# Turned keys masked for all four heads of a tile in one GpSimd operation, and a pipeline with one turn less

## The reference

```
scale, shift = split(cond @ W_emb + b_emb)
xn = rms_norm(x, g_norm) * (1 + scale) + shift
q, k, v = xn @ W_qkv              # 16 heads of 16
q, k = rms_norm(q, g_q), rms_norm(k, g_k)
o = softmax(q k^T / 4) v          # within each sequence, 32 x 32
x = x + o + o @ W_out
```

```
r, z = sigmoid(x W_ir + b + h W_hr + b), sigmoid(x W_iz + b + h W_hz + b)
n = tanh(x W_in + b + r * (h W_hn + b))
h = (1 - z) * n + z * h;  out = x + h
```

## Time and profile before

| | |
|---|---|
| median of 3 runs | 341.93 us (341.85 to 342.36) |
| profiled execution, first to last instruction | 340.0 us |
| attention stage in it, up to the first recurrent product | 191.54 us |
| TensorE, VectorE, ScalarE, GpSimd busy | 323.3, 246.3, 238.0, 224.5 us |

### The profile page before, as it was taken

How to read it: one execution, slowest core, us unless ns; L and a number is a source line. 1 busy time by engine, 2 the same in 40 slices (tenths; PEclk the granted TensorE clock), 3 DMA queues, 4 the chain that set the end, 5 groups by cost and what they waited for, 6 DMA issues and landing times.

```text
span 340.0 us, 12168 instructions
## 1 busy us (share of the span) xinstructions
PE 323.3 (95%) x4177; PEld 293.4 (86%) x4177; DVE 246.3 (72%) x665; ACT 238.0 (70%) x722; POOL 224.5 (66%) x404
## 2 busy tenths in 40 slices
PE   8988899899999999999986999999999999999994
PEld 8767788788888888888874999999999999999994
DVE  3778898888999999999996455565555556555555
ACT  4787777778888788889656566666666666666662
POOL 6787787867777877878778346555555555555542
PEclk9999999999999999999999999999999999999999
DMA  5965237742343333233332221111112111122221
GB/s 202 307 193 151 86 76 234 226 132 85 109 121 113 101 114 99 86 117 116 112 109 65 80 77 48 61 49 62 62 62 62 48 58 50 62 62 62 63 62 33
DMA packets 32205, 34.14 MB, mean 100 GB/s; under 512 B 5286, under 2 KB 26796, under 8 KB 32172
## 3 DMA queue, kind: packets, MB, share of 16 engines
q1 hardware_dynamic: 25868, 26.10, 25.6%
q10 hardware_dynamic: 6304, 7.61, 7.0%
HBM read 12.46 MB, written 8.39 MB: 61 GB/s over the span
## 4 chain that ended last, share of the span: by engine, by line
PE 78%; POOL 7%; SPq 4%; DMA 4%; issue 3%; DVE 3%; ACT 1%; POOLq 0%; DVEq 0%; ACTq 0%
PE bank L1287 38%; PE bank L1244 19%; PE bank L1400 4%; PE bank L1419 4%; PE bank L1388 4%; DMA operands<-operands 4%; PE bank L1531 3%; SPq L414 2%; POOL operands L485 2%; PE bank L1380 2%; SPq L405 2%; PE bank L1250 2%; PE bank L1371 2%; POOL xn L496 1%; POOL xn_lo L531 1%
## 5 line engine op out<-in xcount | busy, mean ns | idle before, releaser
L1287 PE MATMUL bank<-wih_lo,wo_parts 128*128 128x256 f32 x192 | 56.2, 294 | 0.0
L1287 PE MATMUL bank<-wih_hi,wo_parts 128*128 128x256 f32 x192 | 54.6, 285 | 0.2 <-POOL pair_lo L600 0.2
L1287 PE MATMUL bank<-wih_hi,pair_lo 128*128 128x256 f32 x192 | 52.8, 279 | 0.0
L1287 PE MATMUL bank<-wqkv_hi,hT_hi 128*128 128x256 f32 x192 | 52.5, 292 | 0.0
L611 POOL TENSOR_TENSOR operands<-operands,h 128x128 f32<-128x128 f32 x64 | 29.6, 462 | 34.2 <-ACT operands L932 33.4
L1287 PE MATMUL bank<-wqkv_lo,hT_hi 128*128 128x256 f32 x192 | 49.9, 279 | 0.0
L1187 DVE TENSOR_TENSOR operands<-bank,operands 128x128 f32<-128x128 f32 x64 | 18.6, 291 | 39.3 <-ACT operands L929 39.3
L1244 PE MATMUL bank<-wqkv_hi,xn_hi 128*128 128x512 f32 (+1 forms) x124 | 46.4, 375 | 0.2 <-POOL xn_lo L531 0.2
L618 POOL TENSOR_TENSOR w_emb_sb<-h,w_emb_sb 128x256 f32<-128x256 f32 x31 | 22.9, 737 | 30.7 <-DVE h L1204 30.7
L1287 PE MATMUL bank<-wqkv_hi,hT_lo 128*128 128x256 f32 x192 | 42.7, 279 | 0.0
L1244 PE MATMUL bank<-wqkv_hi,xn_lo 128*128 128x512 f32 (+1 forms) x124 | 41.9, 338 | 0.0
(11 more groups left out here) (138 smaller groups left out, 975.2 us busy)
## 6 DMA issues: line engine op xcount, KB each, us to landing
v_diag<-v_rows SPq DMA_DIRECT2D x124, 34.0 KB, 2.1
operands<-operands SPq DMA_DIRECT2D x32, 128.0 KB, 2.1
out_dram<-x ACTq DMA_DIRECT2D x16, 256.0 KB, 2.6
w_emb_sb<-out_dram SPq DMA_DIRECT2D x32, 128.0 KB, 2.1
operands<-operands SPq DMA_DIRECT2D x63, 64.0 KB, 2.0
out_dram<-w_emb_sb SPq DMA_DIRECT2D x31, 128.0 KB, 1.7
x_in<-in_x_dram SPq DMA_DIRECT2D x7, 512.0 KB, 8.6
stage_w<-in_L_cond_W_ih_dram ACTq DMA_DIRECT2D x2, 384.0 KB, 3.4
```

What stands on the lines that cost most here:

```text
L1287: return pe.matmul(dst, moved, gate_columns(weights, k, block), start=False, stop=True, skip_group_check=True)
```

## The change

`mask_keys` writes four copies of the keys in one operation, 128x1024 values: copy m is multiplied by column m of `gqk_place`, which is the gain in the rows of heads with number m modulo 4 and zero elsewhere. `scores` reads these directly; k_diag, its memset and all key copies go, with the two semaphores that counted them. The scores wait for the mask itself, and mask k waits for the scores of group k - 2 in place of key copies. A head's scores now land in another column, so `attention_products` picks another one.

Every stage from the scores on has a lag one smaller, and the last turns' extra pieces move with it. In GpSimd's `body` the mask now stands before the shift. The biases, gate weights and state weights on GpSimd stand one turn earlier, where the mask of the last group keeps turn 37. ScalarE's state_weights keep turns 36 and 37. All value copies are issued by SyncE's queue.

```diff
-PE_X2T, PE_V, PE_S, PE_PV, PE_QKT, PE_OUT, PE_XT, PE_QK = 11, 4, 7, 8, 5, 10, 2, 3
-ACT_LN, ACT_V, ACT_X2T, ACT_QKT, ACT_EXP, ACT_SQX, ACT_SQK, ACT_OT, ACT_XN, ACT_XHAT = 1, 4, 11, 5, 7, 0, 3, 9, 2, 1
-DVE_QKN, DVE_SS, DVE_OT, DVE_MAX, DVE_RCP, DVE_XMOD, DVE_RES, DVE_O, DVE_PT = 4, 3, 8, 6, 7, 1, 9, 7, 6
-POOL_XN, POOL_KEYS, POOL_OT, POOL_XLO, POOL_NEWTON = 3, 6, 10, 3, 1
-SP_V, SP_KEYS = 5, 6
+PE_X2T, PE_V, PE_S, PE_PV, PE_QKT, PE_OUT, PE_XT, PE_QK = 10, 4, 6, 7, 5, 9, 2, 3
+ACT_LN, ACT_V, ACT_X2T, ACT_QKT, ACT_EXP, ACT_SQX, ACT_SQK, ACT_OT, ACT_XN, ACT_XHAT = 1, 4, 10, 5, 6, 0, 3, 8, 2, 1
+DVE_QKN, DVE_SS, DVE_OT, DVE_MAX, DVE_RCP, DVE_XMOD, DVE_RES, DVE_O, DVE_PT = 4, 3, 7, 5, 6, 1, 8, 6, 5
+POOL_XN, POOL_KEYS, POOL_OT, POOL_XLO, POOL_NEWTON = 3, 6, 9, 3, 1
+SP_V = 5
...
-LATE_RESULTS = range(24, 28)
-LAST_TURNS = range(34, 39)
-SHARED_VALUES = (3, 4)
+LATE_RESULTS = range(25, 29)
+LAST_TURNS = range(33, 38)
...
-        KD, KM = 2 * 2 * 2 * D, 2 * 2 * D
-        operands = sb("operands", [P, 14 * D])
-        k_diag = operands[:, 0:KD].rearrange("p (s n r j k) -> p s n r j k", s=2, n=2, r=2, k=T)
-        k_masked = operands[:, KD:KD + KM].rearrange("p (s r f) -> p s r f", s=2, r=2)
+        operands = sb("operands", [P, 2 * NB * D])
+        k_masked = operands[:, :].rearrange("p (s m f) -> p s m f", s=2, m=NB)
...
                 v = group(base, u, SP_V)
-                if v is not None and not (isinstance(v, int) and (v <= 2 or v >= NG - 3)):
+                if v is not None:
                     place_values(v, (u - SP_V) % 4)
...
             def mask_keys(k, slot):
                 pool.wait_ge(qkT_ready, k + 1)
                 if later(k, 2):
-                    pool.wait_ge(k_diag_ready[slot], spread(k - 2, slot, len(KEY_STRIPS)))
+                    pool.wait_ge(s_ps, k - 1)
                 if isinstance(k, int) and k == 0:
                     pool.wait_ge(vec_ready, 3)
                 pool.tensor_tensor(k_masked[:, slot, :, :],
-                                   qkT[:, slot, D:2 * D].unsqueeze(1).broadcast_to([P, 2, D]),
-                                   gqk_parity[:, :].unsqueeze(2).broadcast_to([P, 2, D]),
+                                   qkT[:, slot, D:2 * D].unsqueeze(1).broadcast_to([P, NB, D]),
+                                   gqk_place[:, :].unsqueeze(2).broadcast_to([P, NB, D]),
                                    ALU.mult).then_inc(k_masked_ready, 1)
...
             def body(base, u):
+                k = group(base, u, POOL_KEYS)
+                if k is not None:
+                    mask_keys(k, (u - POOL_KEYS) % 2)
                 g = group(base, u, POOL_XN)
                 if g is not None:
                     shift(g, (u - POOL_XN) % 2)
-                k = group(base, u, POOL_KEYS)
-                if k is not None:
-                    mask_keys(k, (u - POOL_KEYS) % 2)
...
-                if turn_is(base, u, NG + 5):
+                if turn_is(base, u, NG + 4):
                     summed_biases()
                 for i in range(2 * KC):
-                    if turn_is(base, u, NG + (1, 5, 6, 6)[i]):
+                    if turn_is(base, u, NG + (1, 4, 5, 5)[i]):
                         gate_weights(i // 2, i % 2)
-                    if turn_is(base, u, NG + (5, 6, 7, 7)[i]):
+                    if turn_is(base, u, NG + (4, 5, 6, 6)[i]):
                         state_weights(i // 2, i % 2)
...
-            dve.memset(operands[:, 0:KD], 0.0).then_inc(k_diag_clear, 1)
...
             def scores(g, slot):
-                pe.wait_ge(k_diag_ready[slot], spread(g, slot, len(KEY_STRIPS)))
+                pe.wait_ge(k_masked_ready, g + 1)
                 if later(g, 1):
                     pe.wait_ge(logits_ready, g)
                 pe.sem_inc(scores_clear, 1)
                 for c in range(KC):
                     for b in range(GB):
+                        tokens = slice(c * P + T * b, c * P + T * b + T)
                         for i in range(2):
                             rows = slice(2 * PB * i, 2 * PB * i + 2 * PB)
                             last = pe.matmul(s_tiles[i][T * b:T * b + T, c * P:c * P + P]
-                                             .rearrange("p (r n k) -> p n r k", r=2, k=T),
-                                             qkT[rows, slot, c * P + T * b:c * P + T * b + T],
-                                             k_diag[rows, slot, :, :, GB * c + b, :], start=True, stop=True)
+                                             .rearrange("p (m k) -> p m k", k=T),
+                                             qkT[rows, slot, tokens], k_masked[rows, slot, :, tokens],
+                                             start=True, stop=True)
                 last.then_inc(s_ps, 1)
```

More of the change, by code:

```diff
@@ L30 @@
 NB = P // PB
-KEY_STRIPS = ((0, 1), (1, 2), (3, 1))
 BANK = 512
@@ L92, in adaptive_attention_gru @@
         head_rows = sb("head_rows", [P, P // DH])
-        parity = sb("parity", [P, 2])
-        gqk_parity = sb("gqk_parity", [P, 2])
+        place = sb("place", [P, NB])
+        gqk_place = sb("gqk_place", [P, NB])
         mod_scale = sb("mod_scale", [P, KC, NG, GB])
@@ L402, in place_values @@
                 sp.wait_ge(v_ready, v + 1)
-                for b in range(2 if isinstance(v, int) and v in SHARED_VALUES else GB):
+                for b in range(GB):
                     rows = slice(T * b, T * b + T)
@@ L407, in place_values @@
                       .then_inc(v_diag_ready[slot], 16)
[L409 to L416, removed]
-            def body(base, u):
-                if turn_is(base, u, SP_V):
-                    place_values(0, 0)
-                    place_values(1, 1)
-                g = group(base, u, SP_KEYS)
-                if g is not None:
-                    place_keys(g, (u - SP_KEYS) % 2)
-                if turn_is(base, u, SP_KEYS):
-                    place_values(2, 2)
+            def body(base, u):
                 v = group(base, u, SP_V)
-                if v is not None and not (isinstance(v, int) and (v <= 2 or v >= NG - 3)):
+                if v is not None:
                     place_values(v, (u - SP_V) % 4)
-                v = group(base, u, SP_V + 1)
-                if isinstance(v, int) and v >= NG - 3:
-                    place_values(v, (u - SP_V - 1) % 4)
-                if turn_is(base, u, SP_KEYS + 1):
+                if turn_is(base, u, SP_V + 2):
                     load_x(4 * FIRST_SPREAD, NG, x_loaded[FIRST_SPREAD])
-            pipeline(sp, body, NG - 1 + max(SP_V, SP_KEYS))
+            pipeline(sp, body, NG - 1 + SP_V)
             for stored in x2_stored:
@@ L692, in load_gate_weights @@
                 act.dma_start(staged[:, i % KC, :], source[(i % KC) * P:(i % KC) * P + P, :]).then_inc(loaded[i % KC], 16)
-            def place_values(v, first, last):
-                act.wait_ge(v_ready, v + 1)
-                for b in range(first, last):
-                    rows = slice(T * b, T * b + T)
-                    act.dma_start(v_diag[rows, v % 4, b, :, :].rearrange("p h f -> p (h f)"),
-                                  v_rows[rows, v % 4, :, :].rearrange("p h f -> p (h f)"))\
-                       .then_inc(v_diag_ready[v % 4], 16)
-            def last_keys():
-                act.wait_ge(k_masked_ready, NG)
-                first, count = KEY_STRIPS[-1]
-                rows, slot = slice(PB * first, PB * (first + count)), (NG - 1) % 2
-                act.dma_start(k_diag[rows, slot, (len(KEY_STRIPS) - 1) % 2, :, :, :].rearrange("p r j k -> p (r j k)"),
-                              k_masked[rows, slot, :, :].rearrange("p r f -> p (r f)")).then_inc(k_diag_ready[slot], 16)
             def gate_weights(c):
@@ L897, in body @@
                     first_state()
-                for v in SHARED_VALUES:
-                    if turn_is(base, u, v + ACT_V):
-                        place_values(v, 2, GB)
                 for i in range(4):
```

19 lines of the change are left out of this document (6 added, 13 removed).

## The result

The change makes the kernel slower: 348.81 us, median of 4 runs (348.19 to 349.95), against 341.99 for the kernel before, run beside it. The ratio is 1.020, 95% interval 1.017 to 1.022. The forecast of 343.0 us had the sign right and is 5.8 us short; the time lies 2 us above the range. The profiled execution took 348.31 us, its span 346.4. The interval lies clear of 1, so the loss is real, though its size is only about 2%.

The account below looks back on a forecast made before the run. TensorE's 5.056 us a turn bounds the middle; fill and middle give a 3.3 us lead, the drain loses 4.3, so the first recurrent product comes about 1.05 late: span 341.05, plus 1.93 margin, 343.0 us; range 339.3 to 346.8.

Parts of the forecast that it names:

- The fill's term of 0.6 us: Fill, second turn: VectorE's output weights run beside GpSimd and lengthen its turn by 0.6 us.
- spacings of a TensorE at full clock: Drain behind scores 31: old intervals kept, second cast's end at 185.4, first recurrent product at 192.6.
- The wider mask: GpSimd's mask of 1024 columns instead of 512 takes 1.89 us, 0.85 more.
- Does GpSimd become the bound in the middle?: Middle: GpSimd's turn of 4.99 and a ScalarE loop of 5.05 just fit within TensorE's pace of 5.056 us.
- the rival: Middle: GpSimd becomes the bound, through a longer mask or dearer handovers; about 345 to 348.8 us, chance 0.25.
- The copy waits that I took as gained: Middle: 2.07 us of scores waiting for key copies disappear.
- the first rival in its cheapest form: Middle: handovers cost 0.05 to 0.1 more, loops 5.1 to 5.15 us, about 345; chance 0.25 for both forms together.
- The fill: Start of the attention stage: GpSimd turns of 5.0 us, scores 3 at 37.9, 1.65 us ahead of before.
- The drain gives it back: Drain: mask 31 stands behind late weights waiting for ScalarE's cast; scores 31 at 181.2, 0.6 us later than before.
- The first, in its dearest form: Middle: mask of 2.08 to 2.16 us, loops 5.24 to 5.32, total 348.8 us; chance 0.25 for both forms together.
- The second, mask 31 not held up: Drain: state part ready early, scores 31 at 177.9, end at 339.3 us; chance 0.22 for full or most.
- the forecast's own signs of being wrong: Middle scores following at 5.1 us or more, scores 3 starting above 39, or mask 31 starting before 178.

Follow-up runs that it names:

- half a mask: Changed kernel, but the mask writes two of its four slots, the other two zeroed once, so their heads get scores of zero: 341.96 us.
- experiment 6: Changed kernel with GpSimd's late weights in their old turns, VectorE's output weights a turn earlier, gate-weight and bias loads issued by SyncE: 341.42 us.
- Experiment 2: Changed kernel with VectorE's output weights one turn earlier (turn 4 instead of 5): 348.03 us.
- Experiment 1: Changed kernel with GpSimd's biases, gate and state weights back in their turns of before, behind the last group's mask: 344.97 us.
- 3: Changed kernel with GpSimd's late weights back in their old turns and VectorE's output weights a turn earlier: 343.67 us.
- 7: Kernel of experiment 3 with GpSimd's gate piece that stood ahead of mask 28 three turns later: 342.87 us.
- experiment 11: Changed kernel with only the loads of gate weights and biases issued by SyncE instead of ScalarE: 346.84 us.

## Why the prediction was wrong

Four steps of the sum failed, in the order of the span. The fill's term of 0.6 us for the output weights measured 2.4. The middle, from scores 3 to 27, was forecast at TensorE's pace with nothing added, and took 1.65 us more. The drain had the late pieces in the wrong order, 0.95 us. And behind scores 31 it carried over spacings of a TensorE at full clock, 1.4 us.

**The wider mask:** right, 1894 ns for 1.89 us.

**Does GpSimd become the bound in the middle?** I took the pace of 5.056 us "by a hair" and left the rival its own chance. In pace the sum was right: the scores of the changed kernel mostly follow at 5.05. Wrong was to take a pace without slack as free. Scores 3 to 27 took 122.99 us; half a mask, with GpSimd at 0.85 us less a turn, took 121.26. The difference of 1.7 us is made of three things. The first is ScalarE's own issuing of loads: it is listed in the trace of before too, at the same engine, and I didn't ask who waits behind it. Moving it off gave 0.8 us in the middle of the changed kernel, and 2.1 in experiment 6 (scores 7 to 11 in 20.83 us for 22.89). The second is the stall at scores 9 that stays without these issues, 0.5 us, of unknown cause. The third is small and regular: every fourth turn takes 5.2 us. The timeline of GpSimd at one of them in the changed kernel, where the four turns of the loop's body start anew:

```profile
94.27 0.26 POOL L513 TENSOR_TENSOR rs<-newton_a,rs 128x33 f32<-128x33 f32 x1
94.81 1.90 POOL L454 TENSOR_TENSOR operands<-qkT,gqk_place 128x1024 f32<-128x1024 f32 x1 [0.28 <-issue]
```

GpSimd waited 0.28 us for nothing that the profile shows. From scores 11 to 27, (162.86 - 81.57) / 16 = 5.08 us a turn in the changed kernel and (157.96 - 77.13) / 16 = 5.05 with half a mask. That is another 0.5 us. It makes GpSimd the bound in one turn of four, the first rival in its cheapest form. The copy waits that I took as gained (2.07 us) were so in part only: the trace puts 1.65 of them down to copies, and scores 3 to 11 took 42.52 us before and 41.70 now.

**The fill:** the term that failed most. The forecast's turns of 5.0 us on GpSimd held (masks 0 and 1 start at 20.55 and 25.52). The 0.6 us for the output weights, drawn from what the shift lost beside them, is off by a factor of four: GpSimd's turn grew by 2.4 us. I had counted what the shift on GpSimd lost. The one held up is now VectorE, and GpSimd itself waits behind it, through the sum `ss`, ScalarE's root and the Newton steps. Experiment 2 removed it: from scores 0 to 3, 14.90 us for 17.28; 1.0 of these 2.4 us came back as a later start of scores 0 (23.64 for 22.59). For this holding up the Trainium skill has a rule, in SBUF — State Buffer (who interferes with whom): a VectorE instruction with two SBUF inputs contends with a GpSimd instruction that reads SBUF, by an exclusive lock in which the order of issue decides who is blocked. The trace agrees: the pair that starts behind the mask takes 1.99 us for 0.55. I had the row of the shift at 1.13 us and treated it as a toll of fixed size.

The mask's length alone isn't the cause, though. With half a mask VectorE's four steps took 2.78 us for 3.63, and the turn still cost 2.4 us over its neighbour (scores 1 to 2 in 6.49 us, scores 0 to 1 in 4.12), with the same wait:

```profile
30.18 0.24 POOL L508 TENSOR_TENSOR newton_a<-rs 128x33 f32<-128x33 f32 x1 [2.38 <-ACT rs L698]
```

What also changed is the place. In the kernel before no softmax stood ahead of the output weights in VectorE's turn 5, and they began at 22.86. With the pipeline a turn shorter the first softmax stands there, from 23.36 to 26.27. Experiment 2 takes the weights away from the mask and from behind the softmax at once, so no run parts the two.

**The drain gives it back:** the mechanism was right, its order not. Mask 30 starts 7.16 us after scores 28 (forecast 7.15), and the state piece starts 4.41 us after mask 30's end (forecast 4.4). But I had put the gate piece ahead of the state piece, where it would lie in GpSimd's wait. The loop over i does gate and state of each i in turn, so at NG + 4 it is the state piece of i = 0 and then the gate piece of i = 1: 0.95 us later for mask 31, nearly all of the 1.05 on that stretch. Behind scores 31 I carried old spacings over. These came from a TensorE at full clock, and the hold itself takes that away: after 4.50 us without work the granted clock is 0.5, that is 1.2 of 2.4 GHz. The windows:

```profile
184.00:186.00 2.00, 0.00 (x0) 0.01 (x1) 0.00 (x0) 0.00 (x0) 2.00 (x3) 0.52 0.00 0
186.00:188.00 2.00, 1.98 (x64) 1.55 (x64) 0.75 (x2) 0.00 (x0) 2.00 (x3) 0.50 0.00 0
188.00:190.00 2.00, 2.00 (x17) 1.88 (x10) 1.89 (x5) 0.92 (x2) 1.77 (x3) 0.50 0.00 0
190.00:192.00 2.00, 2.00 (x40) 1.65 (x39) 0.70 (x3) 1.63 (x3) 0.76 (x2) 0.78 0.41 134
```

Scores 31 took 1.11 us for 0.67, the second cast started 4.72 us after scores 31 for 3.31 forecast, and this 1.4 is the whole of the 1.33 that the last stretch was off. Experiment 1 bears it out: without the hold the clock stays at 1.00, and its second cast starts 186.22 - 182.91 = 3.31 us after scores 31. With half a mask, where hold and half clock stay, it is 4.72 again.

**The rivals.** The first, in its dearest form, gave 348.8 us, the time that was measured. That is coincidence: it was priced for a mask of 2.08 to 2.16 us and 0.2 us more in each turn of the middle, and neither came; the forecast's range left it out. The right sign is luck in part as well: the drain's mechanism was there, but without it, where the forecast would have had 339.3 us, experiment 1 is still slower than the kernel before. Two of the forecast's own signs of being wrong came: scores 3 start above 39 (39.87), and the middle runs at 122.99 / 24 = 5.12 us on average.

The second, mask 31 not held up, did not happen by itself, but experiment 1 made it so, and it was worth 3.8 us (I had 3.7 between the two cases). Its price was right, and its condition, the cast ahead of the exponentials, was rightly seen as unmet.

What stays open: why the recurrent stage is 0.8 us shorter, the stall at scores 9 that experiment 6 leaves, and how the 2.4 us of the output weights split between the lock and their place behind the softmax.

## What to carry to other kernels

When an operation grows on an engine until its turn is nearly as long as the bound's, price the slack that it eats and not only the pace: list everything that the slack used to hide (issues on another engine's queue, a loop's restart, a setup operation), since each of these becomes visible once. When an operation is made longer or moved, look for every operation on the other engine that contends with it, find out which of the two is held up, and follow who waits behind that one. And before late work is put a turn earlier on a queue, see what it waits for: here one piece waiting for a cast cost more than half of all that was lost, and the same edit with the queues put right is faster than the kernel before (which had no such repairs tried on it).

## What the runs showed of the hardware

- VectorE with two SBUF inputs and GpSimd's mask hold each other up in both directions. In experiment 2 the output weights ran ahead of the first mask instead: VectorE's last one kept its 0.69 us, while mask 0, starting 0.04 us after it, took 2.40 us instead of 1.89.
- GpSimd's product with a factor held over a run of columns costs 1.66 ns a column up to 1024 (618, 1042 and 1894 ns for 256, 512 and 1024), below the 2.18 of two full operands.
- The issue of one and the same bias load (L680) took 0.44 us on ScalarE's queue in the changed kernel, and 1.86, 1.98, 1.48 and 1.43 in experiments 2, 3, 7 and 1; on SyncE's queue it took 0.58, but another bias load there up to 1.33 (experiment 11). Nothing in the profile says why. In experiments 2 and 3 ScalarE's next instruction came 2.00 and 2.12 us late behind these issues.
- TensorE's granted clock was down to half behind 4.50 us of idle in the drain, and behind 4.38 us with half a mask; in the changed kernel it was full again from 192. It was low in the fill of the changed kernel too, where TensorE had worked 1.14 and 0.84 us in the two windows of 2 us before.
